# Per-batch softmax sums in four column tiles, and queries projected transposed and spread by DMA

## The reference, cut to what matters

```
xn     = layernorm(x)
Q      = xn @ Wq + bq             # 16 heads of 32
K, V   = ctx @ Wk + bk, ctx @ Wv + bv      # one head of 32, shared by all query heads
out    = softmax(Q K^T / sqrt(32)) V        # per head, over 2048 keys
x     += out @ Wo + bo
x     += delta-rule memory layer(layernorm(x))   # 4 heads, triangular inverse in 6 levels
x     += top-1 mixture of experts(layernorm(x))  # 16 experts of 512 x 2048 x 512
```

## Time and profile before

| | |
|---|---|
| median of three runs | 2504.54 us |
| the profiled execution | 2506.43 us |
| its span, first to last instruction | 2504.4 us |
| mean granted TensorE clock | 0.943 of full |
| TensorE busy | 2335.0 us (93%) |
| weight loads busy (beside it) | 1552.5 us (62%) |
| VectorE / ScalarE / GpSimd busy | 1370.6 / 1232.2 / 1611.0 us |
| attention and all of `finish` | until about 2080 us; the experts take the rest |

### The profile page before, as it was taken

How to read it: one execution, slowest core, us unless ns; L and a number is a source line. 1 busy time by engine, 2 the same in 40 slices (tenths; PEclk the granted TensorE clock), 3 DMA queues, 4 the chain that set the end, 5 groups by cost and what they waited for, 6 DMA issues and landing times. The chain is left out here.

```text
span 2504.4 us, 36819 instructions
## 1 busy us (share of the span) xinstructions
PE 2335.0 (93%) x13440; PEld 1552.5 (62%) x13440; DVE 1370.6 (55%) x2425; ACT 1232.2 (49%) x2317; POOL 1611.0 (64%) x1307
## 2 busy tenths in 40 slices
PE   5889999999999999999999999999998977999999
PEld 3446565656565656565646565656464547999998
DVE  4655656565656666566656565666655523333333
ACT  3646464546464646454545554555554422333333
POOL 0576767575868586767676767676767724565554
PEclk9889999999998999899989998999898978999999
DMA  4531101010101010112010111110002008999995
GB/s 164 174 117 39 56 35 55 35 55 35 56 35 56 34 55 34 56 35 67 26 69 28 62 35 55 35 55 35 34 1 85 9 13 305 359 348 364 342 372 194
DMA packets 80419, 251.51 MB, mean 100 GB/s; under 512 B 6553, under 2 KB 7193, under 8 KB 72048
## 3 DMA queue, kind: packets, MB, share of 16 engines
q1 hardware_dynamic: 70704, 222.98, 24.7%
q10 hardware_dynamic: 5952, 14.29, 1.6%
q0 software_dynamic: 3584, 11.90, 1.2%
HBM read 224.00 MB, written 25.72 MB: 100 GB/s over the span
## 5 line engine op out<-in xcount | busy, mean ns | idle before, releaser
L932 POOL TENSOR_TENSOR psum<-psum,p 128x512 f32<-128x512 f32 x896 | 1157.0, 1291 | 423.6 <-ACT p L547 344.8
L707 DVE TENSOR_REDUCE mpart<-bank 128x1 f32<-128x512 f32 x1024 | 687.3, 686 | 405.6 <-PE bank L337 398.1
L547 ACT ACTIVATE p<-bank 128x512 f32<-128x512 f32 x1024 | 598.6, 599 | 601.9 <-PE bank L350 593.9
L350 PE MATMUL bank<-qT,kT 97*128 97x512 f32 x1024 | 516.1, 505 | 3.9 <-ACT p L547 3.9
L337 PE MATMUL bank<-kT,qT 96*128 96x512 f32 x1024 | 499.0, 489 | 9.7 <-DVE mpart L707 7.2
L337 PEld LDWEIGHTS bank<-kT,qT 96*128 96x128 f32 x1024 | 206.9, 202 | 252.5 <-issue 142.2
L362 PE MATMUL bank<-p,v 128*32 128x512 f32 x2048 | 302.7, 666 | 0.8 <-ACT p L547 0.7
L350 PEld LDWEIGHTS bank<-qT,kT 97*128 97x128 f32 x1024 | 207.3, 203 | 147.2 <-issue 119.8
L1171 POOL TENSOR_TENSOR w2l<-w,w2h 128x1024 fp32r<-128x1024 f32 x64 | 203.2, 3176 | 75.0 <-PE ebank L1086 54.4
L312 PE MATMUL bank<-cst,w_first 128*128 128x128 f32 x1024 | 158.4, 278 | 20.5 <-DMA w_first<-in_ctx 14.7
L312 PEld LDWEIGHTS bank<-cst,w_first 128*128 128x128 f32 x1024 | 126.9, 143 | 68.1 <-issue 26.2
(11 more groups left out here) (168 smaller groups left out, 3302.6 us busy)
## 6 DMA issues: line engine op xcount, KB each, us to landing
w<-in_w SPq DMA_DIRECT2D x48, 2048.0 KB, 19.7
w_first<-in_ctx SPq DMA_DIRECT2D x64, 1024.0 KB, 4.9
w_first<-in_w SPq DMA_DIRECT2D x16, 2048.0 KB, 12.8
dispatched<-route ACTq DMA_DIRECT2D x17, 513.0 KB, 4.0
dis<-dispatched SPq DMA_DIRECT2D x16, 513.0 KB, 3.5
xin<-in_x SPq DMA_DIRECT2D x16, 256.0 KB, 2.6
xr<-in_x SPq DMA_DIRECT2D x16, 256.0 KB, 5.9
out<-route SPq DMA_DIRECT2D x16, 256.0 KB, 2.0
```

What stands on the lines that cost most here:

```text
L350: e.matmul(B_BANK[u % 2][:], kT[b % 2][0:3 * HD + 1, k * P:(k + 1) * P], qT[b % 2][0:3 * HD + 1, g * 512:(g + 1) * 512], start=True, stop= ...
L547: e.activation(p[n % NP][:], B_BANK[u % 2][:], ACT.Exp).then_inc(p_act.sem, 1)
L707: e.tensor_reduce(mpart[g % 2][:, n:n + 1], A_BANK[(17 * g + n) % 2][:], AX.X, ALU.max).then_inc(max_dve.sem, 1)
L932: e.tensor_tensor(acc[:], first[:], p[(UNITS * b + u) % NP][:], ALU.add).then_inc(psum_pool.sem, 1)
```

## The change

The schedule has no turning of the queries and no per-group sums any more; the steps of `finish` up to `x1` stand some ticks earlier:

```diff
-NORM, XN, XNT, QPROJ, QTURN = 1, 5, 10, 27, [34, 38, 42, 50]
+NORM, XN, XNT, QPROJ, QSEND = 1, 5, 10, 27, 38
-POST = dict(xb=2, oT1=8, x1=11, x1_add=14, norm2=15, xn2=18, ss=19, x12=20, rn=20, xn2T=21, rk=23, V=24, V_copy=27,
-            rkT=30, I=33, XT1=35, X1=39, Vn=93, ...
+POST = dict(xb=2, sums=4, att=5, x1=8, x1_add=11, norm2=12, xn2=15, ss=16, x12=17, rn=17, xn2T=18, rk=20, V=21,
+            V_copy=24, rkT=28, I=32, XT1=34, X1=39, Vn=93, ...
-O_COPY, O_TURN = 1, 4
+O_COPY = 1
```

```diff
-            def turn_out(b, g):
-                e.wait_ge(*oS_act.at(b, g))
...
+            def sums(b):
+                e.wait_ge(*psum_pool.at(b, 15 * HG - 1))
+                e.wait_ge(*oS_act.at(b, HG - 1))
+                if b:
+                    e.wait_ge(*post_dve.at(b - 1, "before"))
+                for out, lhs, src in ((PV_BANK, cst[:, C_ONES, 0:HD], psum), (P_BANK, cst[:, C_STACK, 0:HD], oS)):
+                    for g in range(HG):
+                        ins = e.matmul(out[HD * g:HD * (g + 1), :], lhs, src[g][:], start=True, stop=True)
+                ins.then_inc(sums_pe.sem, 1)
...
-                if t == POST["oT1"]:
-                    e.wait_ge(*o_dve.at(b, "att3"))
-                    transposes(P_BANK, lambda h: cut(att[b % 2], h)).then_inc(post_pe.sem, 1)
+                if t == POST["sums"]:
+                    sums(b)
                 if t == POST["x1"]:
-                    e.wait_ge(*post_act.at(b, "oT1"))
+                    e.wait_ge(*o_dve.at(b, "att"))
# VectorE: out_norm, once a group, goes; in finish:
+                if t == POST["sums"]:
+                    e.wait_ge(*sums_pe.at(b))
+                    e.reciprocal(recip[:], PV_BANK[:]).then_inc(o_dve.sem, 1)
+                if t == POST["att"]:
+                    e.wait_ge(*o_dve.at(b, "recip"))
+                    e.tensor_tensor(turned[:], P_BANK[:], recip[:], ALU.mult).then_inc(o_dve.sem, 1)
# TensorE, weigh: the first of a group waits for the copy before it, of a batch for the reciprocal
-                    e.wait_ge(*(o_dve.at(b, f"att{g - 1}") if g else o_dve.at(b - 1, f"att{HG - 1}")))
+                    e.wait_ge(*(oS_act.at(b, g - 1) if g else o_dve.at(b - 1, "recip")))
# ScalarE, out_sum
+                if b and g == 0:
+                    e.wait_ge(*sums_pe.at(b - 1))
-                e.copy(oS[:], PV_BANK[:]).then_inc(oS_act.sem, 1)
+                e.copy(oS[g][:], PV_BANK[:]).then_inc(oS_act.sem, 1)
# GpSimd, add_weights, k == 1
-                    if 4 * b + g >= 2:
-                        e.wait_ge(*oT_pe.at(0, 4 * b + g - 2))
+                    if b and g == 0:
+                        e.wait_ge(*sums_pe.at(b - 1))
```

```diff
-                if QPROJ <= t < QPROJ + DC:
-                    c = t - QPROJ
-                    ins = e.matmul(KV_BANK[:], xnT[:, c, :], wq[:, c, :], start=c == 0, stop=c == DC - 1)
+                if QPROJ <= t < QPROJ + HG:
+                    cols = slice((t - QPROJ) * P, (t - QPROJ + 1) * P)
+                    for c in range(DC):
+                        ins = e.matmul(KV_BANK[:, cols], wq[:, c, cols], xnT[:, c, :], start=c == 0, stop=c == DC - 1)
-                if t in QTURN:
...
# VectorE, tick 30: one instruction in place of three, and no copies into qT
+                    e.scalar_tensor_tensor(heads(qs[:]), heads(KV_BANK[:]), SCALE,
+                                           bq[:].unsqueeze(2).to_broadcast([P, DC, P]), ALU.mult, ALU.add)
# ScalarE, tick 31
+                    e.copy(qh[:], qs[:]).then_inc(q_act.sem, 1)
# GpSimd, tick 33
+                    e.tensor_tensor(qs[:].bitcast(F32R), qs[:], qh[:].bitcast(F32), ALU.subtract).then_inc(q_pool.sem, 1)
# SyncE, tick 38
+            def send_queries(b):
+                for part, src, ready in ((0, qh, q_act), (1, qh, q_act), (2, qs, q_pool)):
+                    e.wait_ge(*ready.at(b))
+                    for h in range(4):
+                        e.dma_start(
+                            qT[b % 2][part * HD:(part + 1) * HD, :].bitcast(F32).rearrange(
+                                "d (g h t) -> d g h t", g=HG, h=4)[:, :, h, :],
+                            src[h * HD:(h + 1) * HD, :].bitcast(F32).rearrange("d (g t) -> d g t", g=HG)).then_inc(
+                            q_in.sem, 16)
# TensorE, largest, n == 0 (first use at tick 89)
-                    e.wait_ge(*(qT_act if g % 2 else qT_dve).at(b, g // 2))
+                    e.wait_ge(*q_in.at(b, 11))
```

More of the change, by code:

```diff
@@ L137, in attention @@
         qT = [sb(f"qT{i}", [P, NH * P], F32R) for i in range(2)]
-        xin, xnT, qf = sb("xin", [P, D]), sb("xnT", [P, DC, P]), sb("qf", [P, D])
-        q3 = sb("q3", [P, NH, 3 * HD])
+        xin, xnT = sb("xin", [P, D]), sb("xnT", [P, DC, P])
+        qs, qh = sb("qs", [P, D]), sb("qh", [P, D], F32R)
         st1, mv1, rs1 = sb("st1", [P, 6]), sb("mv1", [P, 2]), sb("rs1", [P, 2])
         p = [sb(f"p{i}", [P, 512]) for i in range(NP)]
-        oS, psum = sb("oS", [P, 512]), [sb(f"psum{i}", [P, 512]) for i in range(2)]
+        oS, psum = ([sb(f"{n}{g}", [P, 512]) for g in range(HG)] for n in ("oS", "psum"))
         mpart = [sb(f"mpart{i}", [P, 16]) for i in range(2)]
@@ L192, in attention @@
         b_pe, p_act, pv_pe = count("b_pe", UNITS), count("p_act", UNITS), count("pv_pe", UNITS // 4)
[L193 to L198, removed]
+        psum_pool, oS_act, sums_pe = count("psum_pool", HG * (KB - 1)), count("oS_act", HG), count("sums_pe")
+        o_dve = named("o_dve", "recip att")
+        post_pe = named("post_pe", "x1 xn2T V rkT I X1 Vn oT2 x2 xn3T lg loc")
+        post_act = named("post_act", "ss0 ss1 ss2 ss3 xn2T rk0 rk1 rk2 rk3 V rkT X1 Vn oT2 xn3T eg")
         post_dve = named("post_dve", "x1 st2 mv2 xn2 XT1a MT IT x2 st3 mv3 xn3 lg0 lmax emax cand best oh "
@@ L211, in attention @@
         T_USES = [use for _, use in sorted(
-            [(XNT, ("x", 0))] + [(t, ("q", g)) for g, t in enumerate(QTURN)]
-            + [(t, ("t", k)) for k, t in enumerate(TILE_AT)] + [(t, ("v", c)) for c, t in enumerate(VT_AT)])]
+            [(XNT, ("x", 0))] + [(t, ("t", k)) for k, t in enumerate(TILE_AT)]
+            + [(t, ("v", c)) for c, t in enumerate(VT_AT)])]
         def turn_bank(b, use):
@@ L282, in _ @@
                         load_x(i + 2)
+                    if t == QSEND and i + 1 < B:
+                        send_queries(i + 1)
                     for b, g in groups_at(i, t, MAX_TURN):
@@ L602, in finish @@
                 banks = banks_of(b)
-                if t == POST["oT1"]:
-                    e.wait_ge(*post_pe.at(b, "oT1"))
-                    e.copy(turned[:], P_BANK[:]).then_inc(post_act.sem, 1)
                 if t == POST["ss"]:
```

81 lines of the change are left out of this document (21 added, 60 removed).

## The result

| | before | after |
|---|---|---|
| median of 4 runs each, one chip | 2506.14 us (2502.46 to 2508.91) | 2449.49 us (2448.55 to 2451.53) |
| ratio to before | | 0.9773, interval 0.9761 to 0.9785 |
| span of the profiled execution | 2504.4 us | 2449.7 us |

The change makes the kernel 56.7 us faster. Of all executions behind this document one stood far apart, one of e9's four at 8651.61 us; it is left out of e9's median.

A forecast was written before the change was run, and what follows sets the result against it. TensorE's instruction stream was taken as the bound. A border summed -6.65 + 0.2 + 4.5 + 2.4 - 0.3 = +0.15 us, 14 borders +2; with -9, +4.8 and -1, total -3: 2501 us, range 2450 to 2550.

The forecast's parts named there:

- the clock: Behind the new stall at a border, 4.8 us of work at half clock, costing 2.4 us; bounds 0 to 5.1.
- The rival of little clock loss: The clock does not drop, or for half of what was taken: 2467 to 2484 us; chance 0.16.
- The stream: TensorE's work a batch gets 6.65 us shorter; waits it had covered show again, 0.2 us.
- the rival of tiles in turn: New sums' four tiles run one after another: 4.9 us more a batch, 2575 us; chance 0.04, shared with late queries.
- The stall's mechanism: At a border TensorE waits ahead of x1 for VectorE's 4.41 us reciprocal, normalisation and product: 4.5 us stall.
- GpSimd ... waits with a batch's first addition for the sums: GpSimd waits up to 1 us for the sums at a batch's first addition; it has 38 us free a batch.
- all but 0.7 us in the whole run is streaming: The old per-group sums' 6.8 us a batch is TensorE work and almost no waiting, so it is saved.
- V and the context copy: With finish three ticks earlier, a V wait of 1.1 to 1.3 us replaces one of 1.4: -0.3 us a border.
- Edits costed at zero: SyncE's twelve query DMA issues, 7 us of its queue, delay nothing: 15 us stay free ahead of its next item.
- turn 15: Border where xr lands late and TensorE already stands 8.50 us; the new stall falls into that: -9 us.
- the last batch: No attention beside it: sums to x1 takes 5.2 us instead of 2.35, and two sum sets at half clock: +4.8 us.
- The slower rival: Long half-clock stretch at each border, price 5.1 us, V's wait +0.8: +3.95 us a border, 2551 us; chance 0.21.

The follow-up runs named there:

- e9: Changed kernel with GpSimd's scatter of the routed rows moved from tick 120 to tick 3 of the next batch: 2444.42 us, ratio 0.9742.
- e1: Changed kernel with the queries projected and turned as before, without the query DMAs, some tiles shared to make room: 2498.08 us, ratio 0.9968.
- e15: Changed kernel with three useless matmuls (2.58 us) added to 14 batches at tick 84, where TensorE waits for nothing: 2494.85 us.
- e7: Changed kernel with the division hidden: oS sums first, psum sums into KV_BANK, x1 at tick 12, normalisation ahead of the reciprocal: 2403.69 us, ratio 0.9586.
- e11: e7 with the reciprocal cut into four of 128 columns and GpSimd's scatter at tick 3 of the next batch: 2378.63 us, ratio 0.9475.
- e4: Changed kernel with four useless matmuls (3.4 us) ahead of the wait for x1's operand, all batches but the last two: 2426.71 us, ratio 0.9686.
- e12: e11 with two useless matmuls ahead of TensorE's wait at the routing: 2368.9 us, ratio 0.9438.
- e6: Changed kernel with two useless matmuls ahead of TensorE's wait at the routing: 2461.44 us, ratio 0.981.
- e8: e7 with two useless matmuls ahead of TensorE's wait at the routing: 2425.32 us, ratio 0.9678.
- e5: Kernel before with two useless matmuls ahead of TensorE's wait at the routing (tick 118): 2530.73 us, ratio 1.0093.

## Why the prediction was wrong

**The step that failed is the clock:** "I take 4.8 us of work at half clock, 2.4 us". A border gave -0.8 instead (half of 9.8 - 11.3), a difference of 3.2 us and 44 us over 14 borders. I had priced the stall's new stretch and left the routing's 10.6 us standing as a constant beside it. The new stretch came, but as 3.4 us, and the routing's shrank: of the thirteen whole batches four have 3.4 us there, seven two stretches of 3.4 (one of them from 5 us ahead of the routing's matmul), and only two the old 10.2. A better reading of the rows would not have found it: e1 has the same stall with the old queries, and there the term is +2.3, nearly what I took; e15 has it with 2.58 us more stream, +2.3 again. So the size does not belong to the stall. Nor does the batch period alone set it, since before and e1 both take about 122.8 us a batch with 11.3 and 15.9 us busy at 1.2 GHz. What sets it stays open. The rival of little clock loss bounded the term by zero from below, and so my range did as well; the traces held no reason for that bound. Of the 3.4 us by which a border came out below the forecast, this term is 3.2; less waiting gives 0.6, and a stream that shrank 0.35 less than forecast takes some back.

**The stream was right.** -6.65 + 0.2 against -6.1. The sums take 1.85 us instead of 2.0 and run side by side; the rival of tiles in turn is out.

**The stall's mechanism was right, its size too large**: 3.6 us a border for 4.5. The reciprocal took 3.36 and not 4.41 us, and the normalisation behind it took 0.66 longer than I had it, which hid a part of that error. The slope of the earlier trace rows is (182 - 153) / 3 = 9.7 ns an element, from which I had taken 8.3; between one element and 512 it is (3357 - 153) / 511 = 6.3. The Trainium skill ("VectorE: DVE Perf Modes", "First, the fixed hardware budget") has the reciprocal as an iterative divide with a repeat count of 8, from which I had an estimated 4.27 us at that page's 0.96 GHz. The measured 3.36 is less, and five times the 0.68 of the product next to it: that a reciprocal is the slower operation holds here, the time estimated from the count does not.

**A wait was missed.** "GpSimd ... waits with a batch's first addition for the sums" looks at the wrong end: GpSimd's last additions now hold the sums back, 24.0 us for 6.6, +1.2 a border. I had read GpSimd's 64% as room. The 10.6 us chain from the routing is latency, and the half clock hid it. The prediction's "all but 0.7 us in the whole run is streaming" holds for L372 alone; the rows of L375 had 6.6 us of this wait.

**V and the context copy.** Predicted a wait of 1.2 for one of 1.4. Measured 8.4 - 1.1 and 6.0 - 23.3 over the run, about -0.6 a batch. The routing's own wait also shrank, 22.7 to 15.0. All idle time together: +3.6 a batch, 0.6 less than 4.5 - 0.3.

**Edits costed at zero** were so: SyncE's twelve issues took 8.1 us for the expected 7, far ahead of what comes next.

**The sum over the run.** By the starts of the routing matmuls, 14 borders gave -46 us (predicted +2), turn 15 -5 (-9), the last batch +3 (+4.8), and the first batch -6 (-1). For that last one I had left out a plain term: the first batch's three earlier group sums, 3 x 1.71 us of the earlier trace rows, belong to no border. Together -54.7, the difference of the spans.

**Slips that move nothing.** The slower rival's 3.95 us a border give 2504.5 + 50 = 2554 us and not 2551. The parts named for the forecast's own range give 2488 to 2522 and not 2480 to 2528.

## What to carry over

A stall's own length can be read from queues and durations to a fraction of a microsecond, and streams add. The half-clock time around it does not: here it moved from 9 to 17 us a batch when 2.6 us of work were added far from any wait, so keep it out of a sum as a term and put it into the range, on both sides of zero. When one engine's wait is shortened, look for the next latency chain that the wait (or the slow clock) had covered, by measuring from its start event to its end rather than by busy share. A long instruction on an engine that also frees buffers can cost TensorE even where its own result is not waited for (in e7 the maxima's waits went from 6.1 to 44.4 us in all): cut it, as e11 did.

## What was not expected of the hardware

- Half-clock stretches of 3.4, 6.8 and 10.2 us, and batch periods held 3.4 us apart over one batch or two (116.05, 119.5, 122.9). The runs show that it is so; why the granted clock falls where it does stays open.
- Useless matmuls can make a kernel faster (e4, -23 us; e12 against e11, -10) or slower (e6, +12; e8, +22; e5, +28, by the medians), by what they uncover next.
- A 128x512 reciprocal from PSUM takes 3.36 us, the same in all 16 within 2 ns.
